# Cross-attentions: at even key tiles the side jobs stand behind the value products instead of in front of the couple of maxima

## The chip, the cores and the metric

The kernel runs on one core of a Trainium2 chip. A core has TensorE (PE, matrix products, with a separate row for its weight loads, PEld), VectorE (DVE), ScalarE (ACT), GpSimd (POOL) and SyncE (SP, which issues transfers). Each engine works through its own list of instructions in order, and waits on semaphores that the others raise. The time is the device time of one execution in microseconds (us). The median of three runs is what a version is judged by.

## The reference

A decoder of two layers over x (4 x 512 x 256, float32). Each layer is a self-attention, a cross-attention over a context (4 x 1601 x 192) and a mixture of experts. What the change touches is the two cross-attentions. The first has 8 heads and a mask over the keys, the second has 16 heads and no mask. The head dimension is 64 in both:

```python
q = (x @ W_q).reshape(b, n, HEADS, DIM_HEAD)
k = (context @ W_k).reshape(b, j, HEADS, DIM_HEAD)
v = (context @ W_v).reshape(b, j, HEADS, DIM_HEAD)
sim = jnp.einsum('bihd,bjhd->bhij', q, k) * scale
sim = jnp.where(mask[:, None, None, :], sim, max_neg)      # first layer only
attn = jax.nn.softmax(sim, axis=-1)
out = jnp.einsum('bhij,bjhd->bihd', attn, v).reshape(b, n, INNER)
x = x + out @ W_o + b_o
```

## The kernel before

`cross(layer)` does one cross-attention. Its unit is a group `g`: one batch entry and one pair of heads. The first layer has 4 x 4 = 16 groups (number 0 to 15), the second 4 x 8 = 32 (counted on here as 16 to 47, so that the last is 47). A group goes over its 1601 keys in 13 key tiles `t` of 128 keys (the last of 65), with 512 queries at once.

Per tile, PE makes the scores of the two heads (lines 1164 and 1165, two matmuls each: high and low parts of float32). ACT turns them into exponentials PR (line 1276). POOL adds these up over the tiles in ACC (line 1051). PE multiplies the exponentials with V only at every second tile: at even `t` from 2 on it does the value products of tiles t-2 and t-1 in one go (line 1181, four float32 products that stand as 8 matmuls in the trace).

A softmax needs its maximum ahead of the scores. So while group g is worked on, PE already makes the scores of group g+1 in a coarse form (`maximum`, line 1117). DVE reduces them out of PSUM: in the masked first layer each head alone (line 1334, mask added in the same pass), in the second a couple of both heads in one pass (line 1337). The second layer has a single pair of banks (4 and 5) for these couples once g >= 1. So each couple on PE waits until DVE has reduced the one before it. In the first layer each of two banks serves one head, and a maximum waits for the one before the previous one. `maxima_at(g, t, at)` says at which places of a tile they stand: 0 and 1 behind the scores of the first and second head, 2 behind the side jobs, 3 behind the value products. The second layer has a couple at places 0 and 2 of an odd tile and at place 2 of an even one. The first layer has single maxima at 0, 1, 2 of an odd tile, at 1, 2, 3 of an even one, and at all four at t = 4.

The side jobs, `at(g, t)`, are what else PE has to do for the neighbouring groups, one bank each, in banks 6 and 7 in turn. Job number i waits until job i-2 has been emptied out of its bank:

- `k` (line 1069, 5 matmuls) makes a quarter of the keys of group g+1, at t = 0, 1, 2, 3. ACT copies it to KH (line 1209), and DVE subtracts that copy to get the low part KB (line 1305), which frees the bank.
- `q` (line 1072) makes the queries, at t = 0. DVE finishes it in lines 1310 and 1312 (QA).
- `sum` (line 1089) sums ACC of group g-1 over the keys, at t = 2. ACT empties it (RD, line 1201).
- `v` (line 1081, 10 matmuls) makes values of two key tiles for the next groups. Some groups have four of them (t = 4, 5, 7, 9), some three (t = 5, 7, 9), some seven (every t from 4 to 10), some none.
- `out` (line 1096) is half of group g-1's output projection, at t = 10 and 11. DVE adds it to X (line 1319).
- `row` (line 1085) turns the row of maxima of group g+1, at t = 12.

DVE's list has, for each tile, all maxima first and the jobs of that tile behind them. ACT's has the two exponentials first and then the jobs.

Of the kernel before, what the change touches and what calls it, by code (L numbers as in the profile page):

```python
# [46 lines left out]
def rows_of(kt):  # L47

    return P if kt < KT - 1 else TAIL
# [7 lines left out]
class Core:  # L57
# [756 lines left out]
    def cross(self, layer):  # L814
# [22 lines left out]
        def values_at(g):  # L837


            n = g // 2 + 1  # L840
            if n >= G // 2:
                return []
            jobs = [("v", n, c) for c in range(len(VJ))]
            if 2 * n % pairs == 0:
                return jobs if g % 2 == 1 else []
            return jobs[0:4] if g % 2 == 0 else jobs[4:]

        def at(g, t):

            jobs = []  # L850
            if g + 1 < G:
                jobs += {0: [("k", g + 1, 0), ("q", g + 1, 0)], 1: [("k", g + 1, 1)], 2: [("k", g + 1, 2)],
                         3: [("k", g + 1, 3)]}.get(t, [])
            if g >= 1 and t == 2:
                jobs.append(("sum", g - 1, 0))
            todo = values_at(g)
            for x, tile in zip(todo, {0: (), 3: (5, 7, 9), 4: (4, 5, 7, 9), 7: range(4, 11)}[len(todo)]):
                if tile == t:
                    jobs.append(x)
            if g >= 1 and t in (10, 11):  # L860
                jobs.append(("out", g - 1, t - 10))
            if g + 1 < G and t == 12:
                jobs.append(("row", g + 1, 0))
            return jobs
# [13 lines left out]
        def maxima_at(g, t, *at):  # L878

            return [(g + 1, *x) for w, b in zip(where, blocks) for x in b if w[0] == t and w[1] in at] if g + 1 < G else []  # L880
# [6 lines left out]
        with self.room() as sb:  # L887
# [50 lines left out]
            with self.stage() as (sem, ctx):  # L938
# [21 lines left out]
                def wait_job(eng, job):  # L960

                    i = place[job]
                    eng.wait_ge(job_done[i % 2], i // 2 + 1)
# [90 lines left out]
                def _(pe):  # L1054
                    def job(x):
                        kind, g, c = x
                        i = place[x]
                        J = JB[i % 2]
                        if i >= 2:
                            pe.wait_ge(job_done[i % 2], i // 2)  # L1060
                        if kind == "k":
                            o, w = CHUNKS[c]
                            if c == 0:
                                pe.wait_ge(self.cx_in, cx_base + 16 * (g // pairs + 1))
                                if g >= 1:
                                    pe.wait_ge(kq_in[g % 2], 32 * ((g + 1) // 2))
                            W = WK[:, g % 2, :, :]
                            for n, (u, v) in enumerate(((0, 0), (0, 1), (1, 0), (2, 2), (3, 2))):
                                last = pe.matmul(J[:, 0:w], W[:, u, :], CX[:, v, o:o + w], start=(n == 0), stop=(n == 4))  # L1069
                        elif kind == "q":  # L1070
                            for k in range(CK):
                                last = pe.matmul(J[:, :], WQ[:, g % 2, k, :], HTA[:, g // pairs, k, :], start=(k == 0), stop=(k == CK - 1))
                        elif kind == "v":
                            if c == 0:
                                pe.wait_ge(wv_in, 16 * (g + 1))
                                pe.wait_ge(self.cx_in, cx_base + 16 * (2 * g // pairs + 1))
                            t0, m = VJ[c]
                            for t in range(t0, t0 + m):
                                r, o = rows_of(t), (t - t0) * 2 * P
                                for n, (u, v) in enumerate(((0, 0), (1, 0), (0, 1), (2, 2), (3, 2))):  # L1080
                                    last = pe.matmul(J[0:r, o:o + 2 * P], CX[:, v, t * P:t * P + r], WV[:, u, :],  # L1081
                                                     start=(n == 0), stop=(n == 4))
                        elif kind == "row":
                            pe.wait_ge(m_ready, g + 1)
                            last = pe.transpose(J[:, 0:P], MT[:, :], ident[:, :])
                        elif kind == "sum":
                            pe.wait_ge(summed, 2 * (KT - 1) * (g + 1))
                            for h in range(2):
                                last = pe.matmul(J[h * DH:(h + 1) * DH, :], ones[:, 0:DH], ACC[:, g % 2, h, :], start=True, stop=True)
                        else:  # L1090
                            pe.wait_ge(normed, 2 * g + c + 1)
                            if c == 0:
                                pe.wait_ge(wo_in_sem[g % 2], 16 * (g // 2 + 1))
                            for t in range(2):
                                q = 2 * c + t
                                last = pe.matmul(J[:, t * C:(t + 1) * C], OT[:, q * P:(q + 1) * P], WO[:, g % 2, :], start=True, stop=True)
                        last.then_inc(job_ready[i % 2], 1)
# [52 lines left out]
                    for g in range(G):  # L1150
                        par = g % 2
                        for t in range(KT + 1):
                            for h in range(2 if t < KT else 0):
                                n, r = TP * g + 2 * t + h, rows_of(t)
                                if t == 0 and h == 0:
                                    wait_job(pe, ("q", g, 0))
                                    pe.wait_ge(q_placed, 64 * (g + 1))
                                    pe.wait_ge(k_placed, 64 * (g + 1))
                                    wait_job(pe, ("k", g, NC - 2))
                                    wait_job(pe, ("k", g, NC - 1))  # L1160
                                    pe.wait_ge(row_in, 16 * (g + 1))
                                if n >= 3:
                                    pe.wait_ge(probs, n - 2)
                                pe.matmul(SB[n % 3][0:r, :], KA[:, par, h, t * P:t * P + r], QA[:, par, h, :], start=True, stop=False)  # L1164
                                pe.matmul(SB[n % 3][0:r, :], KB[:, par, h, t * P:t * P + r], QB[:, par, h, :],  # L1165
                                          start=False, stop=True).then_inc(sc_ready, 1)
                                for x in maxima_at(g, t, h):
                                    maximum(*x)
                            for x in at(g, t):
                                job(x)  # L1170
                            for x in maxima_at(g, t, 2):
                                maximum(*x)
                            for s in range(t - 2, t) if t >= 2 and t % 2 == 0 else range(KT - 1, KT) if t == KT else ():
                                r, n = rows_of(s), TP * g + 2 * s
                                pe.wait_ge(probs, n + 2)
                                if g >= 1 and s == 0:
                                    pe.wait_ge(o_done, g)
                                if g % 2 == 0 and s % 2 == 0:
                                    wait_job(pe, ("v", g // 2, s // 2))
                                for h in range(2):  # L1180
                                    last = pe.matmul(OB[h * DH:(h + 1) * DH, :], V[0:r, g % 4, s, h * DH:(h + 1) * DH],  # L1181
                                                     PR[0:r, (n + h) % RING, :], start=(s == 0), stop=(s == KT - 1))
                                last.then_inc(used, 1)
                            for x in maxima_at(g, t, 3):
                                maximum(*x)
                    for x in after:
# [751 lines left out]
```

## Time and profile before

| | us |
|---|---|
| median of 3 runs (3114.33 to 3120.69) | 3120.08 |
| the profiled execution | 3112.38 |
| its span (first to last instruction) | 3110.6 |
| PE busy | 2796.7 (90%) |
| DVE busy | 1857.9 (60%) |
| POOL busy | 1677.5 (54%) |
| ACT busy | 1302.2 (42%) |

The span is all but the whole of the execution: 1.8 us lie around it. The profiled execution was 7.7 us shorter than the median. In the timeline the first cross-attention lies at about 515 to 1240 us, the second at about 1480 to 2970 us. Together they are two thirds of the span. Matmuls are pipelined, and their ends are modelled. So the pace of PE is read from the start of one instruction to the start of the next, not from their lengths.

### The profile page before, as it was taken

What the parts mean: (1) busy time and instruction counts of PE and PEld (TensorE: products, weight loads), DVE (VectorE), ACT (ScalarE), POOL (GpSimd) and SP (SyncE); (2) the same over time, 40 slices, a digit from 0 to 9 for tenths busy, and PEclk for the clock granted to TensorE, in tenths of its full rate; (3) what the DMA queues carried; (4) which work ended last, traced back from release to release, by engine and by line L of the source; (5) the groups of instructions that cost most, each with busy time, mean ns of one, the idle gap of its engine ahead of it and who ended that gap; (6) DMA issues with size and microseconds to landing.
All of it is one profiled execution on the core that took longest, in us unless ns stands there. A gap on an engine that the chain in (4) does not pass through costs nothing. (4 is left out here: it accounts for less than half of the span.)

```text
span 3110.6 us, 38283 instructions
## 1 busy us (share of the span) xinstructions
PE 2796.7 (90%) x12586; PEld 1757.6 (57%) x12586; DVE 1857.9 (60%) x3753; ACT 1302.2 (42%) x2326; POOL 1677.5 (54%) x1421
## 2 busy tenths in 40 slices
PE   7589887999999999586999999999999999999979
PEld 6244445566565664445655566555656556555457
DVE  2677756666767674556555656556556555556456
ACT  1255554544454544123444444444444444444410
POOL 3244404666666667402666656667566666666710
PEclk9799998999999999898999999999999999999979
DMA  9655604233323221103222322323322332222110
GB/s 320 128 163 149 158 6 132 49 98 74 85 69 88 70 58 31 34 1 94 67 50 70 99 59 69 69 51 102 75 51 62 72 87 68 69 55 60 32 58 24
DMA packets 113993, 245.53 MB, mean 79 GB/s; under 512 B 16192, under 2 KB 62530, under 8 KB 112644
## 3 DMA queue, kind: packets, MB, share of 16 engines
q1 hardware_dynamic: 107108, 218.54, 27.4%
q0 software_dynamic: 6176, 24.40, 2.8%
q8 instruction: 102, 1.67, 0.2%
q14 instruction: 95, 0.78, 0.1%
q10 hardware_dynamic: 512, 0.13, 0.0%
HBM read 106.98 MB, written 31.80 MB: 45 GB/s over the span
## 5 line engine op out<-in xcount | busy, mean ns | idle before, releaser
L1051 POOL TENSOR_TENSOR ACC<-ACC,PR 128x512 f32<-128x512 f32 (+1 forms) x1056 | 1330.8, 1282 | 456.8 <-ACT PR L1276 448.6
L1276 ACT ACTIVATE PR<-banks 128x512 f32<-128x512 f32 (+1 forms) x832 | 468.9, 597 | 670.2 <-PE banks L1165 669.2
L1337 DVE TENSOR_REDUCE mx<-banks 128x2 f32<-128x800 f32 (+1 forms) x512 | 504.3, 986 | 394.0 <-PE banks L1117 392.4
L1181 PE MATMUL banks<-PR,V 128*64 128x512 f32 (+1 forms) x2496 | 599.1, 604 | 0.0
L1164 PE MATMUL banks<-QA,KA 128*128 128x512 f32 (+1 forms) x1248 | 535.2, 429 | 11.1 <-DMA QB<-ROW 10.1
L1117 PE MATMUL banks<-KH,QZ 128*128 128x400 f32 (+1 forms) x1536 | 480.6, 372 | 41.2 <-DVE mx L1337 19.3
L1165 PE MATMUL banks<-QB,KB 65*128 65x512 f32 (+1 forms) x1248 | 494.9, 397 | 0.0
L1117 PEld LDWEIGHTS banks<-KH,QZ 128*128 128x128 f32 x1536 | 267.7, 189 | 225.7 <-issue 89.6
L1276 ACT ACTIVATE PR<-banks,small 128x512 f32<-128x512 f32 (+1 forms) x416 | 269.4, 687 | 297.6 <-PE banks L1165 287.4
L1334 DVE CUSTOM_DVE_ANT_0 banks<-banks,maskadd 128x400 f32<-128x400 f32 (+1 forms) x512 | 289.4, 588 | 143.3 <-PE banks L1117 137.1
L1305 DVE TENSOR_TENSOR KB<-banks,KH 64x400 fp32r<-64x400 f32 (+1 forms) x384 | 219.4, 571 | 256.7 <-ACT KH L1209 251.2
L1164 PEld LDWEIGHTS banks<-QA,KA 128*128 128x128 f32 (+1 forms) x1248 | 230.9, 185 | 223.1 <-issue 191.6
L1051 POOL TENSOR_TENSOR ACC<-PR 128x512 f32<-128x512 f32 x96 | 121.1, 1280 | 341.2 <-ACT PR L1276 341.2
L1181 PEld LDWEIGHTS banks<-PR,V 128*64 128x64 f32 (+1 forms) x2496 | 153.7, 136 | 261.1 <-issue 240.9
L1165 PEld LDWEIGHTS banks<-QB,KB 65*128 65x128 f32 (+1 forms) x1248 | 231.4, 185 | 32.0 <-issue 11.0
L1069 PE MATMUL banks<-CX,WK 128*128 128x400 f32 (+1 forms) x960 | 219.3, 359 | 14.2 <-DVE KB L1305 6.2
L1081 PEld LDWEIGHTS banks<-WV,CX 128*128 128x128 f32 (+1 forms) x1560 | 204.6, 184 | 11.6 <-DVE KB L1305 0.2
L1081 PE MATMUL banks<-WV,CX 128*128 128x256 f32 (+1 forms) x1560 | 211.0, 280 | 0.0
L1069 PEld LDWEIGHTS banks<-CX,WK 128*128 128x128 f32 x960 | 177.5, 193 | 47.0 <-DVE QA L1312 18.1
L716 ACT ACTIVATE PR<-banks 128x512 f32<-128x512 f32 x256 | 144.2, 600 | 136.1 <-DVE banks L786 107.9
L1344 DVE RECIPROCAL RD<-RD 128x128 f32<-128x128 f32 x192 | 172.5, 929 | 36.0 <-ACT RD L1201 35.1
L757 DVE CUSTOM_DVE_ANT_0 banks<-banks,strip 128x512 f32<-128x512 f32 x176 | 119.5, 706 | 24.9 <-PE banks L627 23.8
(247 smaller groups left out, 2972.8 us busy)
## 6 DMA issues: line engine op xcount, KB each, us to landing
KA<-KH SPq DMA_DIRECT2D x192, 400.5 KB
CX<-ctx_split SPq DMA_DIRECT2D x8, 2403.0 KB, 10.7
WK<-wk_split SPq DMA_DIRECT2D x48, 256.0 KB, 5.7
WV<-wv_split SPq DMA_DIRECT2D x24, 512.0 KB, 3.6
QA<-QZ SPq DMA_DIRECT2D x96, 128.0 KB
QB<-QZ SPq DMA_DIRECT2D x96, 128.0 KB
first<-in_w_in SPq DMA_DIRECT2D x8, 1024.0 KB, 10.0
second<-in_w_out1T SPq DMA_DIRECT2D x8, 1024.0 KB, 11.3
```

The source lines that it names most:

```text
L1051: pool.tensor_tensor(acc, other, PR[0:r, n % RING, :], ALU.add).then_inc(summed, 1)
L1069: last = pe.matmul(J[:, 0:w], W[:, u, :], CX[:, v, o:o + w], start=(n == 0), stop=(n == 4))
L1081: last = pe.matmul(J[0:r, o:o + 2 * P], CX[:, v, t * P:t * P + r], WV[:, u, :], start=(n == 0), stop=(n == 4))
L1117: pe.matmul(bank_at[:, 0:w], QZ[:, h, t * P:(t + 1) * P], KH[:, o:o + w], start=True, stop=True).then_inc(mx_ready, 1)
L1164: pe.matmul(SB[n % 3][0:r, :], KA[:, par, h, t * P:t * P + r], QA[:, par, h, :], start=True, stop=False)
L1165: pe.matmul(SB[n % 3][0:r, :], KB[:, par, h, t * P:t * P + r], QB[:, par, h, :], start=False, stop=True).then_inc(sc_ready, 1)
L1181: last = pe.matmul(OB[h * DH:(h + 1) * DH, :], V[0:r, g % 4, s, h * DH:(h + 1) * DH], PR[0:r, (n + h) % RING, :], start=(s == 0), stop=(s ...
L1276: act.activation(PR[0:r, n % RING, :], SB[n % 3][0:r, :], ACT.Exp, bias=keybias[0:r, g // pairs, t:t + 1] if masked else 0.0).then_inc(pro ...
L1305: last = dve.tensor_tensor(KB[0:DH, par, h, o:o + w], J[hd, 0:w], KH[hd, o:o + w], ALU.subtract)
L1334: dve.tensor_tensor_reduce(b, b, maskadd[:, g // pairs % 2, o:o + w], 1.0, -BIG, ALU.add, ALU.max, out).then_inc(mx_done, 1)
L1337: dve.tensor_reduce(mx[:, :, t, c], couples[i % 2 if g == 0 else 0][:, :, 0:w], AX.X, ALU.max).then_inc(mx_done, 1)
L1344: dve.reciprocal(part, part).then_inc(inverted, 1)
```

## The change

At even tiles from t = 2 on all side jobs but `row` are issued on PE behind the value products and ahead of the maximum of place 3. Before, they stood between place 1 and place 2. Odd tiles, t = 0 and `row` stay as they were. Nothing is added or taken away, and the lists of ACT, DVE, POOL and SP are the same.

```diff
                             for x in at(g, t):
-                                job(x)
+                                if x[0] == "row" or t < 2 or t % 2:
+                                    job(x)
                             for x in maxima_at(g, t, 2):
                                 maximum(*x)
                             for s in range(t - 2, t) if t >= 2 and t % 2 == 0 else range(KT - 1, KT) if t == KT else ():
...
                                 last.then_inc(used, 1)
+                            for x in at(g, t):
+                                if x[0] != "row" and t >= 2 and t % 2 == 0:
+                                    job(x)
                             for x in maxima_at(g, t, 3):
                                 maximum(*x)
```

What moves is, at t = 2, `k` and `sum` (46 groups have this `k`, 46 this `sum`, 44 both); at t = 4, `v` in 7 groups of the first layer and 15 of the second; at t = 6 and 8, `v` in 3 groups of each layer; and at t = 10, the first `out` in 46 groups, with a `v` ahead of it in 3 of each layer.

PE's list in the second layer at t = 2, before: scores (QA,KA and QB,KB), `k` (CX,WK), `sum` (ACC,ones), the couple of maxima (KH,QZ), the value products (PR,V), the next scores.

```order
L1164 MATMUL banks<-QA,KA 128x512
L1165 MATMUL banks<-QB,KB 128x512
L1069 MATMUL banks<-CX,WK 128x400 x5
L1089 MATMUL banks<-ACC,ones 64x512 x2
L1117 MATMUL banks<-KH,QZ 128x400 x2
L1181 MATMUL banks<-PR,V 64x512 x4
L1164 MATMUL banks<-QA,KA 128x512
```

The same place in the changed kernel:

```order
L1164 MATMUL banks<-QA,KA 128x512
L1165 MATMUL banks<-QB,KB 128x512
L1117 MATMUL banks<-KH,QZ 128x400 x2
L1182 MATMUL banks<-PR,V 64x512 x4
L1069 MATMUL banks<-CX,WK 128x400 x5
L1089 MATMUL banks<-ACC,ones 64x512 x2
L1164 MATMUL banks<-QA,KA 128x512
```

The couple and the value products are now right behind the scores, and `k` and `sum` right ahead of the next scores.

PE's list in the second layer at t = 10, before, with the first `out` (WO,OT) between scores and couple:

```order
L1165 MATMUL banks<-QB,KB 128x512
L1096 MATMUL banks<-WO,OT 128x256 x2
L1117 MATMUL banks<-KH,QZ 128x402 x2
L1181 MATMUL banks<-PR,V 64x512 x4
L1164 MATMUL banks<-QA,KA 128x512
```

The same place in the changed kernel:

```order
L1165 MATMUL banks<-QB,KB 128x512
L1117 MATMUL banks<-KH,QZ 128x402 x2
L1182 MATMUL banks<-PR,V 64x512 x4
L1096 MATMUL banks<-WO,OT 128x256 x2
L1164 MATMUL banks<-QA,KA 128x512
```

Nothing is left between the second head's scores and the couple; `out` follows the value products.

## Rows read from the trace of the kernel before

**Rows 1.** Timeline of PE, second layer, tiles 1 and 2: start, length, instruction, [idle before]

```profile
2044.48 1.08 PE L1069 MATMUL banks<-CX,WK 128*128 128x400 f32 x5
2045.40 0.52 PE L1117 MATMUL banks<-KH,QZ 128*128 128x400 f32 x2
...
2046.46 0.39 PE L1165 MATMUL banks<-QB,KB 65*128 65x512 f32 x1
2046.73 1.17 PE L1069 MATMUL banks<-CX,WK 128*128 128x400 f32 x5
2048.95 1.08 PE L1089 MATMUL banks<-ACC,ones 128*64 128x512 f32 x4 [1.04 <-DVE KB L1305]
2049.96 0.63 PE L1117 MATMUL banks<-KH,QZ 128*128 128x400 f32 x2
2050.52 1.94 PE L1181 MATMUL banks<-PR,V 128*64 128x512 f32 x8
...
2052.38 0.50 PE L1164 MATMUL banks<-QA,KA 128*128 128x512 f32 x1
```

**Rows 2.** Timeline of DVE at the same place

```profile
2046.71 0.99 DVE L1337 TENSOR_REDUCE mx<-banks 128x2 f32<-128x800 f32 x1
2047.74 1.16 DVE L1305 TENSOR_TENSOR KB<-banks,KH 64x400 fp32r<-64x400 f32 x2
```

**Rows 3.** Timeline of PE, second layer, tile 8 of a group without `v` there

```profile
2022.86 0.39 PE L1165 MATMUL banks<-QB,KB 65*128 65x512 f32 x1
2023.41 0.63 PE L1117 MATMUL banks<-KH,QZ 128*128 128x400 f32 x2 [0.16 <-DVE mx L1337]
...
2025.84 0.50 PE L1164 MATMUL banks<-QA,KA 128*128 128x512 f32 x1
```

**Rows 4.** Timeline of PE, second layer, tile 4 of a group with `v` there

```profile
2055.77 0.40 PE L1165 MATMUL banks<-QB,KB 65*128 65x512 f32 x1
2056.01 1.34 PE L1081 MATMUL banks<-WV,CX 128*128 128x256 f32 x10
2057.19 0.52 PE L1117 MATMUL banks<-KH,QZ 128*128 128x400 f32 x2
...
2059.51 0.50 PE L1164 MATMUL banks<-QA,KA 128*128 128x512 f32 x1
```

**Rows 5.** Timeline of PE, second layer, tiles 10 and 11

```profile
2029.26 0.39 PE L1165 MATMUL banks<-QB,KB 65*128 65x512 f32 x1
2029.49 1.03 PE L1096 MATMUL banks<-WO,OT 128*128 128x256 f32 x4
...
2032.68 0.50 PE L1164 MATMUL banks<-QA,KA 128*128 128x512 f32 x1
...
2034.09 1.03 PE L1096 MATMUL banks<-WO,OT 128*128 128x256 f32 x4
2034.87 0.64 PE L1117 MATMUL banks<-KH,QZ 128*128 128x402 f32 x2
```

**Rows 6.** Timeline of PE, first layer, tile 2: last scores and next scores

```profile
942.44 0.39 PE L1165 MATMUL banks<-QB,KB 65*128 65x512 f32 x1
...
948.10 0.39 PE L1164 MATMUL banks<-QA,KA 128*128 128x512 f32 x1
```

**Rows 7.** Timeline of DVE at the same place: end of the maximum of tile 1

```profile
943.36 0.14 DVE L1334 DVE_READ_ACCUMULATOR2_ANT mx<- 128x1 f32 x1
```

**Rows 8.** Timeline of PE, first layer, tile 4, with `v` and (next group) without

```profile
905.77 0.40 PE L1165 MATMUL banks<-QB,KB 65*128 65x512 f32 x1
...
910.00 0.39 PE L1164 MATMUL banks<-QA,KA 128*128 128x512 f32 x1
...
952.09 0.39 PE L1165 MATMUL banks<-QB,KB 65*128 65x512 f32 x1
...
953.79 0.45 PE L1117 MATMUL banks<-KH,QZ 128*128 128x400 f32 x1 [1.13 <-DVE mx L1334]
...
956.33 0.40 PE L1164 MATMUL banks<-QA,KA 128*128 128x512 f32 x1
```

## The prediction

> **What bounds the kernel now.** I read the busy shares of the page first (PE 90%, the others at most 60%), then the timeline of PE and of DVE tile by tile in both cross-attentions. PE's list is the bound there: ACT, POOL and DVE have gaps in each tile, and PE has small ones at fixed places. The timeline is regular to some hundredths of a us from group to group, so one group of each kind stands for all, with its count.
>
> The yardstick is the stretch from the start of the second head's last score matmul (line 1165) to the start of the next tile's first (line 1164). In it stand all that the change moves. Two kinds of PE waits are in such stretches. At t = 2 `sum` waits 1.04 us for DVE's KB of the job two before it [rows 1]. At even tiles where nothing stands between the scores and the couple, the couple waits for DVE to finish the previous couple [rows 3]. The change takes jobs away from in front of the couple. So the question in each place is how much of the job was free, because it lay over that second wait.
>
> **t = 2, second layer.** Before, the stretch is 2046.46 to 2052.38, 5.92 us [rows 1]. After the change the couple is next behind the scores. It needs the reduction of the couple of tile 1, which DVE begins at 2046.71 (it is busy with QA until then) and ends at 2047.70 [rows 2]. Nothing ahead of it changes, so it ends there again. DVE's KB ends at 2048.90 [rows 2], and `sum` starts at 2048.95 [rows 1], so a release costs 0.05 to 0.06. The couple then starts at 2047.76. From there: couple to values 0.56 (2049.96 to 2050.52), values 1.86 (2050.52 to the next scores at 2052.38), `k` 0.92 (2044.48 to 2045.40), `sum` 1.01 (2048.95 to 2049.96) [rows 1]. I add 0.10 for the first matmul behind the values: the score matmul that stands there now is 0.50 long instead of 0.40 [rows 1, 4]. Sum: 2047.76 + 0.56 + 1.86 + 0.10 + 0.92 + 1.01 = 2052.21, against 2052.38. The wait of `sum` goes, and a wait of the couple of 1.07 (2046.69 to 2047.76) takes its place: 0.17 is gained, not 1.04. 30 groups have it so: 30 x -0.17 = -5.1. Bounds -0.35 (the switch costs nothing and `sum`, which no longer restarts after a wait, is 0.1 shorter) and +0.10 (the float32 products cost more next to each other): -10.5 to +3.
>
> Who is late next there? KB of this `k` comes some 3.5 us later than now and frees the bank for the `k` of t = 3. It starts at 2050.28; by my estimate its product is ready 1.2 later, ACT's copy takes 0.5 and KB 1.16 [rows 2], which ends near 2053.2. The `k` of t = 3 has its turn some 1.4 behind the new 2052.21, at 2053.6. So I put it at nothing; 30 x 0.2 is the most that I see. ACT's exponentials of tile 3 stand behind the copies of `k` and `sum`, which now end as these scores are ready. PE needs them only three scores later.
>
> **t = 2, first layer.** Before 942.44 to 948.10, 5.66 us [rows 6]. The maximum of place 2 now comes right behind that of place 1 and waits for the one of tile 1. DVE is through with that at 943.50 [rows 7]. So it starts at 943.55. Then about 0.3 for it (a single maximum, estimated at half of the couple's 0.56), 1.86, 0.10, 0.92, 1.01 [rows 1], and 0.3 for the maximum of place 3: 948.04. Nothing is won or lost in 14 groups, +-2 in all.
>
> The first group of each layer has `k` but no `sum` at t = 2, so no wait goes, while `k` (0.92, [rows 1]) comes onto the path behind a wait: 2 x 0.8 = +1.6.
>
> **t = 4, 6, 8, second layer.** Without `v` a stretch is 2.98 (2022.86 to 2025.84), its couple starting 0.55 behind the scores; with `v` in front it is 3.74 (2055.77 to 2059.51), and `v` itself takes 1.18 (2056.01 to 2057.19) [rows 3, 4]. So `v` now costs 0.76, and 0.42 of it lies over the couple's wait. Behind the values nothing waits that it could lie over: 2.98 + 1.18 = 4.16, +0.42. It stands 15 times at t = 4 and 3 times each at t = 6 and 8: 21 x 0.42 = +8.8.
>
> **t = 4, first layer.** With `v` the stretch is 4.23 (905.77 to 910.00), without it 4.24 (952.09 to 956.33) [rows 8]. The maximum of place 2 waits for that of place 0, which DVE reaches only behind KB; 1.13 of wait is seen where `v` is missing [rows 8]. There `v` is free now. Behind the values it is not: 7 x 1.18 = +8.3. At t = 6 and 8 of this layer the maxima alternate between two banks and are not waited for without `v`; moving it changes nothing.
>
> **t = 10.** Second layer, before 2029.26 to 2032.68, 3.42 [rows 5]. After, the couple waits as at t = 8, a stretch of 2.98 [rows 3], and `out` is added. Its four matmuls take 0.78 up to the couple at t = 11 [rows 5], a switch from score to float32 matmuls included; behind the values, which are float32 too, I take 0.70 (an estimate, bounds 0.55 and 0.90). So 2.98 + 0.70 - 3.42 = +0.26, 30 times: +7.8, bounds +3.3 and +14. First layer, 14 times: no wait comes or goes. `out` and a maximum change places, put at nothing, +-0.2 each, +-2.8.
>
> In the last group of each layer there are no maxima, so jobs and values change places at no cost.
>
> **Sum.** -5.1 + 0 + 1.6 + 8.8 + 8.3 + 7.8 + 0 = +21.4 us. Against the profiled execution 3112.38 + 21.4 = 3133.8. That one was 7.7 below the median of 3120.08, so the median comes to 3120.08 + 21.4, 3141.5. All low ends together give +8, all high ends +41.
>
> A rule of the Trainium skill speaks to the same thing. The couple's wait in [rows 3] shows that two couples in one pair of banks, with only scores between them, do not overlap with their reduction. The page "Perfetto Trace Analysis", section "Matmuls", says that independent groups of matmuls should rotate through different PSUM banks so that the emptying of one overlaps the matmuls of the next. The change takes jobs of other banks out from between groups of the same banks. By the rule without the rows I would price that at the first layer's t = 6, 8 and 10 too (20 places, by 0.32 as in the second: +6, so +28). The rows show these without a wait, and I stay with the rows.
>
> **Rivals.**
> - *It is faster: the couple does not wait at t = 2.* The wait of `sum` (1.04 in the second layer) then goes for good. For it speaks that the change shortens PE's list in front of everything that DVE does next. Against it: the reduction of tile 1 stands behind QA in DVE's list and ends at 2047.70 whatever PE does [rows 2]. If DVE ended it 1.07 earlier in 30 groups, and its like 0.7 earlier in the first layer's 14, the change would gain a further 32 + 10: 21.4 - 42 = -21, 3099. The sign changes if the couple's wait at t = 2 is under some 0.6 instead of 1.07. I give it 5%.
> - *The jobs are paid back later.* With `v` and `out` behind the values, DVE gets that time to catch up, and a later wait of the same group shrinks by as much. That would need waits of 0.4 and more in the odd tiles that follow, and the groups that have `v` at an even tile have another `v` in each of the odd tiles 5, 7 and 9, over which their couples do not wait now. Price: the 8.8 and 8.3 come back, +4.3, 3124. 10%.
> - *The float32 products cost more side by side.* Each job behind the values, in front of scores, drains PE once more. Priced at 0.15 (half as much again as the 0.10 above) at some 90 places: +14, 3155. The rows show only the one switch of 0.10 [rows 1, 4]. 12%.
> - *The order does not change:* excluded by the two orders shown.
>
> **How the numbers follow.** The forecast of 3142 with its own spread of +12 to +31 has 73%, the three rivals 5, 10 and 12. The range reaches from 3127 to 3155: the forecast's spread, the dearer case up to its price and a part of the paid-back case. A measurement of this kernel can tell 0.2% from no change, 6.2 us. Faster by more than that: 0.05. Within it: the paid-back case with a little of the forecast's low end, 0.11. Slower: 0.84.
>
> **What would show it.** In the trace of the changed kernel: at t = 2 of the second layer no wait for KB in front of `sum`, and a wait for the reduction (line 1337) of about 1 us in front of the couple, with a stretch of about 5.76 instead of 5.92. At t = 4 with `v` 4.2 instead of 3.7 in the second layer, 5.4 instead of 4.2 in the first. At t = 10 of the second layer 3.7 instead of 3.4. PE's total idle for DVE KB in front of line 1089 should fall from some 38 us to next to nothing, that for lines 1334 and 1337 in front of line 1117 rise by about as much or more. I am wrong if the stretches at t = 2 fall by half a us or more, or if an odd tile gets shorter by what its neighbour loses.

## The result and the profile after

The changed kernel takes 3138.86 us in the median of five executions (3135.97 to 3154.09), against 3114.33 for the kernel before in the runs beside it (3104.01 to 3120.69). The ratio is 1.0087, with a 95% interval of 1.0054 to 1.0120: slower by 0.9%, some 27 us by the ratio. The profiled execution has a span of 3138.6 us, 28.0 more than before. Of all executions reported here one stands apart, the profiled one of `e1_sum`: it took 8363.29 us, with PE busy for 8229.3 of them, and the ratios leave it out.

| | before | after |
|---|---|---|
| span, us | 3110.6 | 3138.6 |
| first score matmul of line 1165 in the first cross-attention, at us | 516.7 | 511.0 |
| last one in the second cross-attention, at us | 2956.9 | 2984.1 |
| between the two | 2440.2 | 2473.1 |

Between the first score and the last, the trace after is 32.9 us longer. Ahead of it, it is 5.7 us shorter, in code that the change does not touch. Compared stretch by stretch (from one last score matmul to the next), 30.6 of the 32.9 is at the even tiles 2 to 10. Another 1.6 has nothing to do with the change: in group 4 at t = 0, behind a wait of 1.27 for a DMA, the granted clock was 0.50 for some 3 us, which no other run has there.

The timeline of PE in the second layer at t = 2, after (start, length, instruction, idle before and its releaser), answers to [rows 1]:

```profile
2062.83 0.39 PE L1165 MATMUL banks<-QB,KB 65*128 65x512 f32 x1
2064.13 0.63 PE L1117 MATMUL banks<-KH,QZ 128*128 128x400 f32 x2 [0.91 <-DVE mx L1341]
2064.69 1.94 PE L1182 MATMUL banks<-PR,V 128*64 128x512 f32 x8
2066.56 1.19 PE L1069 MATMUL banks<-CX,WK 128*128 128x400 f32 x5
2067.67 1.08 PE L1089 MATMUL banks<-ACC,ones 128*64 128x512 f32 x4
2068.68 0.50 PE L1164 MATMUL banks<-QA,KA 128*128 128x512 f32 x1
```

And DVE there, which answers to [rows 2]:

```profile
2062.30 0.76 DVE L1316 SCALAR_TENSOR_TENSOR QA<-banks,qscale,QZ 64x512 fp32r<-64x512 f32 x1
2063.08 0.99 DVE L1341 TENSOR_REDUCE mx<-banks 128x2 f32<-128x800 f32 x1
2064.11 1.16 DVE L1309 TENSOR_TENSOR KB<-banks,KH 64x400 fp32r<-64x400 f32 x2
```

`sum` has no wait for KB any more. The couple has one instead: it starts 1.30 behind the scores, as DVE ends the reduction of tile 1 at 2064.07. The stretch is 5.85 where it was 5.92. Over the whole execution, PE's idle time in front of `sum` that KB ended falls from 38.2 us to nothing, and its idle time in front of maxima that DVE's reductions ended rises from 36.3 to 86.8.

PE in the second layer at t = 4 with `v`, which answers to [rows 4], and at t = 10, which answers to [rows 5]:

```profile
2072.05 0.39 PE L1165 MATMUL banks<-QB,KB 65*128 65x512 f32 x1
2072.70 0.60 PE L1117 MATMUL banks<-KH,QZ 128*128 128x400 f32 x2 [0.26 <-DVE mx L1341]
2073.23 1.94 PE L1182 MATMUL banks<-PR,V 128*64 128x512 f32 x8
2075.10 1.45 PE L1081 MATMUL banks<-WV,CX 128*128 128x256 f32 x10
2076.38 0.39 PE L1164 MATMUL banks<-QA,KA 128*128 128x512 f32 x1
...
2093.18 0.40 PE L1165 MATMUL banks<-QB,KB 65*128 65x512 f32 x1
2093.73 0.64 PE L1117 MATMUL banks<-KH,QZ 128*128 128x402 f32 x2
2094.29 1.94 PE L1182 MATMUL banks<-PR,V 128*64 128x512 f32 x8
2096.16 1.13 PE L1096 MATMUL banks<-WO,OT 128*128 128x256 f32 x4
2096.94 0.58 PE L1164 MATMUL banks<-QA,KA 128*128 128x512 f32 x1
2097.36 0.40 PE L1165 MATMUL banks<-QB,KB 65*128 65x512 f32 x1
```

The stretches are 4.33 (before 3.74) and 3.76 (before 3.42). To the next L1165, which takes in the first score matmul (0.33 to 0.42 behind float32 products, 0.23 behind others), they grew by 0.49 and 0.41.

PE in the first layer at t = 4 with `v`, which answers to [rows 8]:

```profile
909.18 0.40 PE L1165 MATMUL banks<-QB,KB 65*128 65x512 f32 x1
909.42 0.35 PE L1117 MATMUL banks<-KH,QZ 128*128 128x400 f32 x1
910.88 0.45 PE L1117 MATMUL banks<-KH,QZ 128*128 128x400 f32 x1 [1.11 <-DVE mx L1338]
911.26 1.94 PE L1182 MATMUL banks<-PR,V 128*64 128x512 f32 x8
913.13 1.44 PE L1081 MATMUL banks<-WV,CX 128*128 128x256 f32 x10
914.41 0.35 PE L1117 MATMUL banks<-KH,QZ 128*128 128x400 f32 x1
914.59 0.39 PE L1164 MATMUL banks<-QA,KA 128*128 128x512 f32 x1
```

The maximum starts 1.70 behind the scores, just as in the groups without `v` before, and `v` then takes its time on the path: 5.41 instead of 4.23.

### The profile page after: what moved, and what is told of

Its sections match the earlier page's. It is cut to its first block and busy times, and to the rows that moved or that the text cites. A ratio compares the mean times of both kernels' runs of the same rounds, so it can differ in the third digit from the quotient of the medians.

```text
span 3138.6 us, 38283 instructions
## 1 busy us (share of the span) xinstructions
PE 2810.2 (90%) x12586; PEld 1750.6 (56%) x12586; DVE 1855.0 (59%) x3753; ACT 1302.1 (41%) x2326; POOL 1676.8 (53%) x1421
## 5 line engine op out<-in xcount | busy, mean ns | idle before, releaser
L1117 PE MATMUL banks<-KH,QZ 128*128 128x400 f32 (+1 forms) x1536 | 474.0, 369 | 94.5 <-DVE mx L1341 54.0
L1165 PE MATMUL banks<-QB,KB 65*128 65x512 f32 (+1 forms) x1248 | 495.2, 397 | 0.0
L1165 PEld LDWEIGHTS banks<-QB,KB 65*128 65x128 f32 (+1 forms) x1248 | 231.5, 186 | 32.9 <-issue 11.0
L1213 ACT ACTIVATE KH<-banks 128x400 fp32r<-128x400 f32 x192 | 97.9, 510 | 201.0 <-PE banks L1069 200.9
```

Source lines behind the costliest of these rows:

```text
L1117: pe.matmul(bank_at[:, 0:w], QZ[:, h, t * P:(t + 1) * P], KH[:, o:o + w], start=True, stop=True).then_inc(mx_ready, 1)
```

## The experiments

The theory: each side job gave cover to a wait of the maximum of place 2, and behind the value products it covers nothing. At t = 2 the wait of `sum` is only exchanged for that one. Rivals: the loss comes from changes between kinds of matmuls, or the jobs are paid back later. The diffs are against the kernel before, but for `e8_after_middle`. Lengths of stretches are from the runs' traces, against the trace of before.

### The change again, and its three parts

`e0_after` is the changed kernel. The other three send only some jobs behind the values; the condition is `t == 2` in `e2_t2`, `x[0] == "v" and t % 2 == 0` in `e3_v`, `x[0] == "out" and t == 10` in `e4_out`:

```diff
                             for x in at(g, t):
-                                job(x)
+                                if not (t == 2):
+                                    job(x)
...
                                 last.then_inc(used, 1)
+                            for x in at(g, t):
+                                if t == 2:
+                                    job(x)
                             for x in maxima_at(g, t, 3):
```

> The changed kernel once more, as the sum of the next three. Read tile by tile, its trace is 32 us longer than before in the two cross-attentions, and 6 us shorter ahead of them. Theory (each part costs the cover that it gave): again +30 to +33 in the cross-attentions. If the 6 us ahead of them are chance from run to run, they are not there again.

> Only the jobs of t = 2 (k and sum) stand behind the value products; v and out stay in front. Theory: the wait of sum for KB (1.04) goes and a wait of the couple (or single maximum) takes its place; about +1 us in all, within 0.2% of before. Rival 'the couple does not wait': -40 us. Rival 'jobs behind the values drain PE each time': +8 or more.

> Only v at t = 4, 6, 8 and 10 stands behind the value products. Theory: the full 1.18 at t = 4 of the first layer (7 groups, +8.3), 0.4 to 0.5 at each of 21 places of the second (+9.6), together +18 us. Rival 'paid back later': within 5 us of before.

> Only the first out (t = 10) stands behind the value products. Theory: the couple's wait of 0.32 comes bare and out costs more there than estimated: 0.41 in 30 groups of the second layer, nothing in the first: +12 us. By the forecast's term it would be +8; by 'paid back later' 0. With e2_t2 and e3_v it should add up to e0_after.

Measured, all beside the same runs of before (median 3111.96):

| | median, us | ratio | 95% interval | cross-attentions by stretches, us |
|---|---|---|---|---|
| `e0_after` | 3149.03 | 1.0119 | 1.0094 to 1.0144 | +30.7 |
| `e2_t2` | 3114.25 | 1.0005 | 0.9992 to 1.0017 | -0.6 |
| `e3_v` | 3133.26 | 1.0065 | 1.0050 to 1.0080 | +20.0 |
| `e4_out` | 3124.57 | 1.0044 | 1.0025 to 1.0062 | +10.8 |

The parts add up to 1.0114 in ratios and +30.2 in stretches: the change is the sum of its parts to within half a us. The jobs of t = 2 are a wash, so that no gain was there for the others to eat up. In `e3_v`, `v` costs 1.17 or 1.18 at t = 4 of the first layer, 0.47 to 0.49 at 15 places of the second and 0.41 or 0.42 at 6. In the first group it cost 2.8: PE waited there for 1.13, and the granted clock was 0.50 for the 3 us that followed. So 1.6 of the +20.0 is the clock, and +18.4 is left, against the +18 expected. In `e4_out`, `out` costs some 0.42 in 27 groups of the second layer, but nothing in the three groups that have a `v` in front of the couple: a job that still stands there gives the cover. With both behind the values, as in the changed kernel, these three places cost 0.36 each. Nothing is paid back at odd tiles. The 5.7 us ahead of the cross-attentions were chance: in `e0_after` the first score comes at 520.2, in `e4_out` at 510.7.

### `sum` alone behind the values

```diff
                             for x in at(g, t):
-                                job(x)
+                                if not (x[0] == "sum"):
+                                    job(x)
...
+                            for x in at(g, t):
+                                if x[0] == "sum":
+                                    job(x)
                             for x in maxima_at(g, t, 3):
```

> Only sum (t = 2) stands behind the value products; k stays in front and covers the couple's wait, v and out stay as before. Theory: of the two waits at t = 2 neither is left. Second layer: couple at 1.29 behind the scores as in the first group, then 0.56, 1.86, 1.0 for sum: 4.7 instead of 5.9, -1.1 to -1.2 in 30 groups. First layer: -0.6 to -0.8 in 14 groups, unless the k of t = 3 waits longer. Together -40 to -45 us, faster by 1.3%. Rival 'jobs behind the values drain PE each time': half of it.

Measured: 3057.29, ratio 0.9819 (0.9798 to 0.9840), faster by 1.8%. No trace of this run is read; the same kernel ran again.

> The kernel of e1_sum once more, for a trace in which its tile 2 can be read. In the trace of e5_sum_middle, which holds the same edit, the stretch of t = 2 is 4.57 (second layer, before 5.92) and 4.72 (first layer, before 5.66). So in the cross-attentions -40 and -13, some -53 to -57 us in all, and nothing changed at t = 4, 6, 8 and 10.

Measured: 3060.45, ratio 0.9819 (0.9795 to 0.9842). The timeline of PE at t = 2, second layer, in `e10_sum_again`:

```profile
2022.82 0.39 PE L1165 MATMUL banks<-QB,KB 65*128 65x512 f32 x1
2023.09 1.17 PE L1069 MATMUL banks<-CX,WK 128*128 128x400 f32 x5
2024.12 0.63 PE L1117 MATMUL banks<-KH,QZ 128*128 128x400 f32 x2
2024.67 1.94 PE L1182 MATMUL banks<-PR,V 128*64 128x512 f32 x8
2026.44 1.03 PE L1089 MATMUL banks<-ACC,ones 128*64 128x512 f32 x4
2027.40 0.50 PE L1164 MATMUL banks<-QA,KA 128*128 128x512 f32 x1
```

Neither wait is left. `k` lies over the wait of the couple, which starts at 1.30 behind the scores as in the changed kernel; the values lie over the wait of `sum`. The stretch is 4.58 instead of 5.92. Over all groups t = 2 gives 39.8 us in the second layer and 12.8 in the first, 52.6 of some 56. The expectation of 40 to 45 was too low: `sum` took its place with 0.96 and the values in front of it 1.77, where [rows 1] have 1.01 (behind a wait) and 1.86, and in the first layer 0.9 a group was won, not 0.6 to 0.8. So `sum` right behind the values is no dearer than apart but cheaper, the contrary of what the rival "drain each time" says of `sum`.

### `k` alone behind the values

The same edit with the condition `x[0] == "k" and t == 2`.

> The other half of the change at t = 2: only k stands behind the value products, sum stays in front. Theory: sum still waits for KB until 2.49 behind the scores, with less in front of it, so the couple starts where it did, at 3.5, and k comes on top: 5.92 + 1.0 to 1.1, or +1.0 in 30 groups of the second layer. In the first layer sum starts at 2.1 as before and k comes on top too, +1.0 in 14, unless the k of t = 3 then waits less. Together +40 to +47 us, slower by 1.4%. If the change's own +1 us at t = 2 were two jobs of no effect each, this would be within 0.2% of before.

Measured: 3212.25, ratio 1.0309 (1.0280 to 1.0339), slower by 3.1%, twice what was expected. The stretches at t = 2 grew by 0.90 in most groups (1.0 was expected). Two things had been left out. At t = 3 of the second layer the next `k` now waits for KB, which with its new edges makes another 0.86 in each of 30 groups. The second layer's first group, which has no `sum`, grows by as much, there through a wait of the couple (+26.6 in all). And in 13 groups t = 2 is 1.6 to 3.1 longer still. PE in one of the three dearest:

```profile
2090.36 0.39 PE L1165 MATMUL banks<-QB,KB 65*128 65x512 f32 x1
2092.85 1.98 PE L1089 MATMUL banks<-ACC,ones 128*64 128x512 f32 x4 [2.10 <-DVE KB L1309]
2094.76 1.04 PE L1117 MATMUL banks<-KH,QZ 128*128 128x400 f32 x2
2095.72 3.68 PE L1182 MATMUL banks<-PR,V 128*64 128x512 f32 x8
```

The same matmuls take twice as long as in [rows 1]. Busy time and granted clock (PEclk) in the stretches around it:

```profile
core 0: us, PE busy (x), PEclk, DMA share, GB/s
2090.30:2092.80 2.50, 0.45 (x2) 0.96 0.88 203
2092.85:2099.30 6.45, 6.45 (x14) 0.50 0.00 0
```

PE stood idle for 2.10 us, and the granted clock is 0.50, the level of 1.2 GHz, from its next matmul to the end of the value products; `k` behind them is at full pace again. In the other ten groups the clock is 0.50 for about half as long, mostly under the value products, and 1.6 to 1.7 is lost. Of the 92.3 us by which the stretches grew, `k` on the path is 0.90 x 44 = 39.6 and 1.6 in the two first groups, t = 3 is 26.6, and the low clock is 25.7; all other tiles together are 1.2 shorter.

### The maximum of place 2 between the value products

`e5_sum_middle` is `e1_sum` with this besides:

```diff
+                            middle = t in ((4,) if masked else (4, 6, 8)) and not at(g, t)
-                            for x in maxima_at(g, t, 2):
+                            for x in maxima_at(g, t, 2) if not middle else ():
                                 maximum(*x)
...
                                 last.then_inc(used, 1)
+                                for x in maxima_at(g, t, 2) if middle and s == t - 2 else ():
+                                    maximum(*x)
```

`e8_after_middle` is the changed kernel with the same lines, and `middle = t in ((2, 4) if masked else (2, 4, 6, 8, 10))`.

> e1_sum, and besides, where an even tile has no side job (t = 4, 6, 8 of the second layer, 72 places; t = 4 of the first, 8 places), the maximum of place 2 stands between the two tiles' value products. Theory: its wait for DVE (0.32 to 0.40, and 1.13 in the first layer) is covered by half of the value products; the extra change between kinds of products costs back about 0.2. -0.1 to -0.2 at 72 places and -0.9 at 8: a further -14 to -22 us beyond e1_sum. If the wait is not the cause, the added change makes it slower than e1_sum by 10 or more.

> The changed kernel (all jobs behind the values), but the maximum of place 2 between the two tiles' value products at every even tile of the second layer and at t = 2 and 4 of the first. Theory: the loss of the change is the bare wait of that maximum; with the wait covered it goes: t = 2 -0.8 in 30 and -0.6 in 14 groups, the other even tiles of the second layer -0.1 to -0.2 in 124 places, t = 4 of the first -1 in 15: some -60 us against the changed kernel, so -30 against before. Rival 'the jobs are dear because they stand next to float32 products': it stays above before.

Measured: `e5_sum_middle` 3045.28, ratio 0.9778 (0.9757 to 0.9799). `e8_after_middle` 3092.89, ratio 0.9934 (0.9912 to 0.9956). The first is the fastest kernel of this study, by 2.2%. PE at t = 8 of the second layer in it, which answers to [rows 3]:

```profile
1980.34 0.40 PE L1165 MATMUL banks<-QB,KB 65*128 65x512 f32 x1
1980.67 1.08 PE L1183 MATMUL banks<-PR,V 128*64 128x512 f32 x4
1981.68 0.63 PE L1117 MATMUL banks<-KH,QZ 128*128 128x400 f32 x2
1982.24 1.08 PE L1183 MATMUL banks<-PR,V 128*64 128x512 f32 x4
1983.25 0.50 PE L1164 MATMUL banks<-QA,KA 128*128 128x512 f32 x1
```

There is no wait left, yet the stretch is 2.91 instead of 2.98: of the 0.32 that the couple had waited, some 0.25 goes for the extra change between kinds of products (the values take 1.01 twice instead of 1.86 in one, and start 0.10 later behind the scores). At t = 4 of the first layer, where the wait was 1.13, 0.86 is won in each of 8 groups. In the second layer 0.14 is won a place at t = 4 and 0.07 at t = 6 and 8. Together that is -13.1 beyond `sum` alone, just short of the expected -14 to -22.

`e8_after_middle` undoes the loss and more: its stretches come to -22.3 against before and some -54 against the changed kernel, where -60 was expected. Most of it is at t = 2: 5.02 in the second layer instead of the changed kernel's 5.85. The jobs stand next to the float32 products as they do in the changed kernel, so the rival that blames that falls for t = 2. At t = 4 of the first layer it falls for 0.86 of the 1.18 that `v` costs; 0.32 is left. For the rest of the second layer it does not fall: with the wait covered `out` at t = 10 still costs 0.36 and `v` 0.34, against 0.41 to 0.49. There the wait that is covered and the extra change of products that it takes to cover it are nearly of one size. That the jobs lose their 0.4 by the bared wait is read from the trace after, in which the couple waits where the job stood; no run separates it from the changes of products.

## Why the prediction was right

Predicted were 3141.5 us (3127 to 3155), slower, by +21.4. Measured were 3138.86 and a ratio that makes +27 on 3114.33, in the range and nearest to the likeliest case. The trace is less kind: its +32 lies just above the +12 to +31 that the forecast gave its own sum, half as much again as the sum said. The terms, against the stretches of the profile after (to the next L1165):

| term | forecast, us | measured, us |
|---|---|---|
| t = 2, second layer, 30 groups | -5.1 | -2.5 |
| t = 2, first layer, 14 groups | 0 | +1.3 |
| first group of each layer, t = 2 | +1.6 | +1.6 |
| `v`, second layer, 21 places | +8.8 | +9.6 |
| `v` at t = 4, first layer, 7 groups | +8.3 | +8.3 |
| `out` at t = 10, second layer, 30 groups | +7.8 | +12.4 |
| `out` at t = 10, first layer | 0 | below 0.3 |
| t = 3 in the second layer's first group | not named | +0.9 |
| low clock in group 4 at t = 0, by chance | not named | +1.6 |
| t = 12, both layers | not named | -1.2 |
| all cross-attention tiles | +21.4 | some +32 |

The mechanism held in each place: which wait goes, which comes in its place, and where a job had been free. The sign of t = 2, on which the case turned, was shown by `e2_t2` (ratio 1.0005), and its reason by `e1_sum` and `e9_k`: sending back only `sum` gains 1.8%, sending back only `k` loses 3.1%. The rival "the couple does not wait" fell (the couple starts 1.30 behind the scores in the trace after, as forecast); "paid back later" fell with `e3_v` and `e4_out`. "Float32 products cost more side by side" fell only in part. Next to each other they are not dearer: `sum` right behind the values was cheaper. But its price, 0.15 at 90 places or +14, is not far from the +9 or so by which the moved jobs cost more than forecast.

The mis-sized terms are two. At t = 10 I took the stretch as 2.98 + 0.70 for `out`. It measured 0.78, as at t = 11 in [rows 5], so the 0.08 that I took off because `out` follows float32 products was not there. And the next scores' first matmul took 0.42 behind it instead of 0.33 behind the values: 0.41 a group, not 0.26. At t = 2 I added 0.10 for `k` behind the values. From `k` to `sum` it took 1.11 (2066.56 to 2067.67), 0.19 more than the 0.92 of a `k` among products of its kind. The change between float32 products and those of the split (high and low) parts is paid twice there, once on each side of `k`. In both places I had left out the edge behind the moved job.

Three smaller things. `v` at t = 4 of the second layer costs 0.48 and not 0.42, because the couple waits 0.1 longer there than at t = 8, where I had read the stretch without `v` ([rows 3]). In the second layer's first group, which has no `sum`, the late KB of `k` comes in front of a reduction at t = 3, and the next couple waits 0.60 for it; I had put the lateness of KB at nothing. And the low ends of my terms add up to +6.7, not to +8.

The median came out nearer than the sum deserved: by the medians side by side the change costs 24.5 us in the first comparison and 37 in `e0_after`, and the median of before that I started from, 3120.08, was 5 to 8 above those of the later runs (3111.96 to 3115.2).

The Trainium skill's rule, in "Perfetto Trace Analysis", section "Matmuls", that groups of matmuls should rotate through PSUM banks so that one is emptied under the next, priced the first layer's t = 6, 8 and 10 too. The trace after shows no wait there: the maxima of the two heads go to two banks, and here that was enough. Where the rows did show the wait, the rule's sign was right.

## What to carry to other kernels

A job between two users of the same bank can be cover. Before it is moved, look for the wait that it hides, which the trace of the running kernel shows only where the job is missing. When two jobs stand in front of a wait, ask for each by itself what it covers and what it waits for: here one was cover and the other the waiter, moving both was worth nothing, and moving only the waiter was worth 1.8%. Price a moved block by both of its new edges, the change of products ahead of it and the one behind it.

## What the runs showed of the hardware

In `e9_k` a wait of PE of 1.5 to 2.1 us was followed by a granted clock of 0.50, in the midst of a stretch with the clock at 1.00, in 13 of 44 groups and not in the others. It was so in 11 of the 30 groups with 2.05 to 2.10 us of wait and in 2 of the 14 with 1.50 to 1.56. In three of them the low clock lasted for 6.45 us of matmuls, in ten for about half of that. It followed shorter waits too, but seldom: 1.13 in one group of `e3_v`, 1.27 in one of the changed kernel. The kernel before, with 1.04 in front of `sum` in 30 groups [rows 1], had the clock at 1.00 in both cross-attentions but for their first 6 us. So a wait on PE can cost more than its length, by 1.6 to 3.1 us each time here, and how often it does is not shown to follow from its length alone.

A change of PE from float32 products to the products of split parts (scores, keys, maxima) and back had a price of its own: 0.19 around `k` behind the values, and some 0.25 where the couple stands between two value products.
